# Graph attention with layer norm: the main loop written out, its leaky relu moved onto VectorE alone

## The reference

```
XW = X @ W
s_col = XW @ a[0,:f];  s_row = XW @ a[0,f:]
Z1 = leaky_relu(s_row[:,None] + s_col[None,:], 0.01)
den = exp(Z1)
num = A @ den                                  # 2048 x 2048 x 2048
att = where(num != 0, den / num, 0)            # division by where(num != 0, num, 1)
out = layernorm(x + A @ (att @ XW))
```

## Time and profile before

| | |
|---|---|
| median of 3 runs | 464.31 us (463.53 to 465.45) |
| span of the profiled execution | 463.2 us |
| TensorE busy | 331.5 us (72%) |
| VectorE busy | 317.1 us (68%) |
| ScalarE busy | 198.6 us (43%) |
| GpSimd busy | 188.3 us (41%) |
| chain that ended last | TensorE 50%, VectorE 24%, GpSimd 10% |

### The profile page before, as it was taken

The page is one execution under the profiler, slowest core; times in us unless marked ns, Lnnn a source line. Parts: engine busy times, 40 slices in busy tenths (PEclk is TensorE's granted clock), DMA queues, the critical chain, the costliest instruction groups (busy, mean ns, idle before and its releaser), DMA issues.

```text
span 463.2 us, 7133 instructions
## 1 busy us (share of the span) xinstructions
PE 331.5 (72%) x2214; PEld 166.9 (36%) x2215; DVE 317.1 (68%) x497; ACT 198.6 (43%) x308; POOL 188.3 (41%) x164
## 2 busy tenths in 40 slices
PE   4853718759784333579999999999999840399960
PEld 2553614435561111224343444433444320144420
DVE  0579989998938673869898999975999900201026
ACT  1110022123313474668777777766777840100010
POOL 4000024355555788557454544642556457000000
PEclk9875555697998569689999999999999985599995
DMA  3030043435552325500000000000000041300002
GB/s 111 0 92 2 3 139 95 131 99 178 183 178 74 102 69 150 156 1 0 2 1 0 0 0 0 0 0 0 0 0 0 1 123 52 96 1 0 0 24 68
DMA packets 13877, 24.68 MB, mean 53 GB/s; under 512 B 2080, under 2 KB 8608, under 8 KB 13728
## 3 DMA queue, kind: packets, MB, share of 16 engines
q0 software_dynamic: 5632, 18.88, 13.4%
q1 hardware_dynamic: 8224, 5.51, 4.1%
HBM read 21.23 MB, written 3.15 MB: 53 GB/s over the span
## 4 chain that ended last, share of the span: by engine, by line
PE 50%; DVE 24%; POOL 10%; issue 5%; DMA 5%; ACT 3%; POOLq 0%; SPq 0%; DVEq 0%; ACTq 0%
PE ps L395 17%; PE ps L364 12%; PE ps L424 9%; DVE D L573 5%; DVE D L575 4%; POOL xws L249 3%; POOL d_b L277 3%; PE ps L390 3%; DMA stage<-adjT,perm 3%; PE ps L354 2%; DVE Alo L728 2%; DVE D L579 2%; POOL Alo L233 2%; DVE xws L576 2%; POOL stage L223 2%
## 5 line engine op out<-in xcount | busy, mean ns | idle before, releaser
L267 POOL TENSOR_TENSOR crow<-rrow,cj 128x512 f32<-128x512 f32 x64 | 79.3, 1239 | 79.0 <-DVE crow L751 77.7
L395 PE MATMUL ps<-Ahi,D 128*128 x248 | 87.2, 382 | 2.9 <-issue 1.4
L354 PE MATMUL ps<-Ahi,E 128*96 128x512 f16 x128 | 57.1, 499 | 44.5 <-POOL Alo L233 25.2
L223 POOL DMA_INDIRECT stage<-adjT,perm x32 | 38.9, 1216 | 101.2 <-DVE rs L599 54.6
L754 DVE TENSOR_TENSOR tmp<-crow,tmp 128x512 f32<-128x512 f32 x64 | 65.4, 1022 | 18.3 <-ACT tmp L503 16.5
L364 PE MATMUL ps<-stage,xwp 128*128 128x512 f32 x128 | 71.6, 641 | 2.4 <-DVE stage L741 2.4
L448 ACT CAST Ahi<-stage 128x1024 f16<-128x1024 f32 x32 | 33.2, 1045 | 62.7 <-DMA stage<-adjT,perm 62.2
L424 PE MATMUL ps<-Ahi,D 128*128 128x512 f16 x128 | 40.2, 393 | 24.0 <-DVE D L766 24.0
L501 ACT ACTIVATE tmp<-ps 128x512 f32<-128x512 f32 x64 | 38.1, 595 | 37.7 <-PE ps L397 37.7
L751 DVE SCALAR_TENSOR_TENSOR crow<-crow 128x512 f32<-128x512 f32 x64 | 49.5, 773 | 0.0
L395 PE MATMUL ps<-Alo,D 128*128 x124 | 47.2, 380 | 0.0
(11 more groups left out here) (137 smaller groups left out, 445.5 us busy)
## 6 DMA issues: line engine op xcount, KB each, us to landing
tmp<-xT SPq DMA_DIRECT2D x1, 1024.0 KB, 4.8
d_xw<-stage SPq DMA_DIRECT2D x1, 1024.0 KB, 5.1
xws<-d_b SPq DMA_DIRECT2D x2, 512.0 KB, 4.8
out<-crow SPq DMA_DIRECT2D x4, 256.0 KB, 2.3
stage<-adjT,perm POOLq DMA_INDIRECT x32
xws<-d_xw,perm POOLq DMA_INDIRECT x16
d_b<-crow,ranku POOLq DMA_INDIRECT x16
stage<-wT SPq DMA_DIRECT2D x1, 64.0 KB, 1.9
```

What stands on the lines that cost most here:

```text
L223: nc.gpsimd.indirect_dma_start(out=st[n % NG], out_offset=None, in_=rows, in_offset=bass.IndirectOffsetOnAxis(ap=perm[:, 0, h, b:b + 1], a ...
L267: nc.gpsimd.tensor_tensor(q_t[c % 2], rrow[:, c * W:(c + 1) * W], cj[:, u:u + 1].to_broadcast([P, W]), ALU.add).then_inc(S["q_ready"], 1)
L354: mm = nc.tensor.matmul(ps[0:R, c, :], E[:, e, b, :], a[:, b, c * W:(c + 1) * W], start=(b == 0 and i == 0), stop=(b == NB - 1 and i == 2))
L395: nc.tensor.matmul(num[c], D[:, d, bass.ds(slot, 1), :], a[:, bass.ds(k, 1), c * W:(c + 1) * W], start=False, stop=(i == 2), skip_group_ch ...
```

## The change

TensorE, ScalarE and VectorE get all 16 block columns written out with J as a constant; only the loop over k stays a hardware loop. GpSimd has no part in the main loop any more.

VectorE uses that leaky_relu(r + s) = s + max(r, 0.01 r - 0.99 s). `r01` = 0.01 `rrow` is made once by ScalarE in two halves ahead of the loop, `shift` = -0.99 `cs` once by VectorE. The missing s goes into the bias of the Exp: `ebias` = `cs` + the old bias. One `scalar_tensor_tensor` for a chunk replaces GpSimd's addition and VectorE's old leaky relu. It is placed one chunk ahead: `lz` of chunk t+1, the subtraction of t, `att` of t-1.

The weights matmul is cut into two halves of 256 columns, the first ahead of the k loop, the second behind it in place of the matmul of zeros. `add_bt` reads `xws` itself; the copies into `xwp` go, and the wait for `xws_in` goes from ScalarE to TensorE. The loads of lo and hi stand at the head of every J.

```diff
-                        nc.tensor.matmul(num[c], wgt[0:R, bass.ds(J * P, P)], sums[0:R, c * W:(c + 1) * W],
-                                         start=True, stop=False, skip_group_check=True)
+            for J in range(NB):
+                lo, hi1 = ends_of(J)
+                for c in range(NC):
+                    t = J * NC + c
...
+                    nc.tensor.matmul(num[c][:, 0:HW], wgt[0:R, J * P:(J + 1) * P], sums[0:R, o:o + HW],
+                                     start=True, stop=False, skip_group_check=True)
+                    with pe.Fori(lo, hi1) as k:
...
-                        nc.tensor.matmul(num[c][:, 0:1], z16[:, :], z16[:, 0:1], start=False, stop=True,
-                                         skip_group_check=True).then_inc(S["num_ready"], 1)
+                    nc.tensor.matmul(num[c][:, HW:W], wgt[0:R, J * P:(J + 1) * P], sums[0:R, o + HW:o + W],
+                                     start=False, stop=True, skip_group_check=True).then_inc(S["num_ready"], 1)
+                    if t >= LAG:
+                        add_bt(t - LAG)
```

```diff
 # ScalarE
-            act.wait_ge(S["xws_in"], 16 * NB)
+            wait_lo(act, 2 * NB - 1)
+            act.wait_ge(S["d_z"], NS)
+            for h in range(2):
+                nc.scalar.mul(r01[h], rrow[:, h * H:(h + 1) * H], SLOPE).then_inc(S["r01_sb"], 1)
             act.wait_ge(S["d_lo"], len(BATCH))
+            act.wait_ge(S["shift_sb"], 2)
...
-                            nc.scalar.copy(xwp[:, u, :], xws[:, bass.ds(J * FEAT, FEAT)]).then_inc(S["xwp_ready"], 1)
...
-                nc.scalar.activation(L_t[c], L_t[c], ACT.Exp, bias=sc[:, 4:5]).then_inc(S["exp_done"], 1)
+                nc.scalar.activation(L_t[c], L_t[c], ACT.Exp, bias=ebias[:, J:J + 1]).then_inc(S["exp_done"], 1)
```

```diff
 # VectorE
+            V.tensor_scalar(shift[:, :], cs[:, :], SLOPE - 1.0, None, ALU.mult).then_inc(S["shift_sb"], 1)
+            V.tensor_scalar(ebias[:, :], cs[:, :], sc[:, 4:5], None, ALU.add).then_inc(S["shift_sb"], 1)
...
-                        V.scalar_tensor_tensor(lz_t[c % 2], q_t[c % 2], SLOPE, q_t[c % 2], ALU.mult, ALU.max).then_inc(S["lz_ready"], 1)
+                V.scalar_tensor_tensor(lz_t[t % 2], r01[c // 2][:, c % 2 * W:(c % 2 + 1) * W], shift[:, J:J + 1], rrow[:, c * W:(c + 1) * W],
+                                       ALU.add, ALU.max).then_inc(S["lz_ready"], 1)
```

More of the change, by code:

```diff
@@ L91, in graph_attention_layernorm @@
         a2s = sb("a2s", [P, 2])
-        xwp = sb("xwp", [P, 2, FEAT])
+        shift = sb("shift", [P, NB])
+        ebias = sb("ebias", [P, NB])
         ends = sb("ends", [P, 2, NB])
@@ L121, in graph_attention_layernorm @@
         st = [stage[:, g * H:(g + 1) * H] for g in range(NG)]
-        q_t = [crow[:, 0:W], crow[:, W:2 * W]]
-        lz_t = [crow[:, 2 * W:3 * W], crow[:, 3 * W:4 * W]]
+        lz_t = [crow[:, i * W:(i + 1) * W] for i in range(2)]
+        r01 = [stage[:, 0:H], crow[:, H:N]]
         L_t = [tmp[:, i * W:(i + 1) * W] for i in range(NC)]
@@ L251, in _ @@
                             in_offset=bass.IndirectOffsetOnAxis(ap=perm[:, 1, 2, b:b + 1], axis=0)).then_inc(S["xws_in"], 16)
[L254 to L272, removed]
             for b in range(NB):
@@ L357, in _, with add_bt @@
                     mm.then_inc(S["p_sums"], 1)
-            def add_bt(J, u, c, first, last):
-                t = J * NC + c
+            def add_bt(t):
+                J, c = divmod(t, NC)
                 if c == 0:
-                    pe.wait_ge(S["xwp_ready"], J + 1)
+                    pe.wait_ge(S["xws_in"], 16 * NB)
                 pe.wait_ge(S["att_ready"], t + 1)
-                nc.tensor.matmul(bt[c], xwp[:, u, :], att[c], start=first, stop=last).then_inc(S["bt_added"], 1)
+                nc.tensor.matmul(bt[c], xws[:, J * FEAT:(J + 1) * FEAT], att[c], start=(J == 0), stop=(J == NB - 1)
+                                 ).then_inc(S["bt_added"], 1)
             pe.wait_ge(S["w_lo"], 1)
@@ L368, in _ @@
             LAG = 3
+            HW = W // 2
             def ends_of(J):
[L372 to L379, removed]
-                    else:
[L381 to L389, removed]
-                        nc.tensor.matmul(num[c], wgt[0:R, bass.ds(J * P, P)], sums[0:R, c * W:(c + 1) * W],
-                                         start=True, stop=False, skip_group_check=True)
[L392 to L396, removed]
-                        nc.tensor.matmul(num[c][:, 0:1], z16[:, :], z16[:, 0:1], start=False, stop=True,
-                                         skip_group_check=True).then_inc(S["num_ready"], 1)
-                        if not (first and u == 0 and c < LAG):
-                            pu, pc = divmod(u * NC + c - LAG, NC)
-                            add_bt(J0 + pu, pu % 2, pc, first and pu == 0, last and pu == 1)
@@ L486, in exp_of @@
                 act.wait_ge(S["sub_done"], t + 1)
-                nc.scalar.activation(L_t[c], L_t[c], ACT.Exp, bias=sc[:, 4:5]).then_inc(S["exp_done"], 1)
[L489 to L496, removed]
-                            nc.scalar.copy(xwp[:, u, :], xws[:, bass.ds(J * FEAT, FEAT)]).then_inc(S["xwp_ready"], 1)
[L498 to L510, removed]
+                nc.scalar.activation(L_t[c], L_t[c], ACT.Exp, bias=ebias[:, J:J + 1]).then_inc(S["exp_done"], 1)
+            for t in range(NB * NC):
+                c = t % NC
+                act.wait_ge(S["num_ready"], t + 1)
+                if t >= NC:
+                    act.wait_ge(S["att_ready"], t - NC + 1)
+                nc.scalar.activation(L_t[c], num[c], ACT.Square, scale=1.0 / 256).then_inc(S["sq_done"], 1)
+                act.wait_ge(S["sq_done"], t + 1)
+                nc.scalar.activation(L_t[c], L_t[c], ACT.Ln, bias=epst[:, 1:2]).then_inc(S["ln_done"], 1)
+                if t:
+                    exp_of(t - 1)
@@ L738, in att_of @@
+            def att_of(t):
+                c = t % NC
                 dve.wait_ge(S["exp_done"], t + 1)
-                if not first:
+                if t >= NC:
                     dve.wait_ge(S["bt_added"], t - NC + 1)
                 V.scalar_tensor_tensor(att[c], num[c], 1.0 / 256, L_t[c], ALU.mult, ALU.mult).then_inc(S["att_ready"], 1)
[L743 to L750, removed]
-                        V.scalar_tensor_tensor(lz_t[c % 2], q_t[c % 2], SLOPE, q_t[c % 2], ALU.mult, ALU.max).then_inc(S["lz_ready"], 1)
[L752 to L761, removed]
+            lz_of(0)
+            for t in range(NB * NC):
+                c = t % NC
+                if t + 1 < NB * NC:
+                    lz_of(t + 1)
+                dve.wait_ge(S["lz_ready"], t + 1)
+                dve.wait_ge(S["ln_done"], t + 1)
+                V.tensor_tensor(L_t[c], lz_t[t % 2], L_t[c], ALU.subtract).then_inc(S["sub_done"], 1)
+                if t:
+                    att_of(t - 1)
```

38 lines of the change are left out of this document (25 added, 13 removed).

## The result

The changed kernel takes 451.74 us (median of 4 runs, 450.72 to 452.32) against 464.07 us (463.53 to 465.45). The ratio is 0.9715, 95% interval 0.969 to 0.9741: 12.3 us less. The forecast was 455.4 with a range of 452 to 460. The profiled execution took 450.72 us, the shortest of the four, and its span is 449.0.

The account below looks back on a forecast made before the run. The prediction took TensorE to bound the main loop, VectorE close behind. Its terms -7.0 - 1.1 - 0.9 + 1.6 - 1.5 summed to -8.9 against the 463.2 us span, 454.3; plus 1.1 for the median, 455.4 us, range 452 to 460.

Parts of the forecast that it names:

- late starts and single waits go: TensorE's main loop: twelve late k-loop starts vanish when written out, -7.0 us, and three single waits, -1.1.
- halves for zeros: Weights matmul halves replacing the zeros: -0.015 us a chunk over 60 chunks, -0.9 us, between -1.8 and +3.
- the loop's start: ScalarE's two multiplications ahead of the first Square delay add_bt of chunk 0, +1.1, loads +0.5: +1.6 us (+0.6 to +3.1).
- the loop's end: Block column 15: last Exp at 369.6 instead of 370.99, plus two waits of 0.1: -1.5 us (0 to -2).
- the range's lower end: Whole kernel: 452 us, with stalls gone, the halves at -1.6 and the start at +0.6.
- the 1.1 us of the median: Whole kernel: the median was taken to lie 1.1 us above the profiled span, making 454.3 into 455.4.
- Written out: TensorE's loop with constant J: all twelve late starts in chunks 0 and 3 of even J go, -7.0 us.
- VectorE and GpSimd: Main loop: without GpSimd's 64 additions VectorE needs 2.06 to 2.23 us a chunk, not 2.48; gains slack and 1.1 us of waits.
- rival C: Loop's start: TensorE idles some 2.3 us ahead of add_bt of 0, its clock falls, costing 1.5 us: 456.9; chance 0.17.
- A: Head of each J: loads of lo and hi stay exposed, 7.7 of 8.2 us stay: 463.1; chance 0.09.
- B: Entry of the k loop: TensorE's sequencer becomes the bound, slower; 474 if half of 64 chunks do; chance 0.05.
- D: TensorE's late starts come from the k loop's dynamic start; about half stay, +4 us: 459.4; chance 0.11.

Follow-up runs that it names:

- e2: The changed kernel with one whole weights matmul ahead of the k loop and the one-column matmul of zeros behind it again: 457.16 us, ratio 0.9836.
- e3: The changed kernel with the whole weights matmul back and a matmul of 256 columns of zeros behind the k loop: 458.35 us, ratio 0.9869.
- e1: The kernel before with only the weights matmul in halves, the second replacing the zeros, inside the hardware loop over pairs: 464.67 us, ratio 1.0005.
- e5: The kernel before with only TensorE's loop over pairs written out; zeros, load order and GpSimd's part stay: 455.53 us, ratio 0.9831.
- e6: The changed kernel with TensorE's part, xwp and its copies as before, so the new leaky relu stays and GpSimd is idle: 463.01 us, ratio 0.9996.
- e10: The kernel before with TensorE's loop written out and the weights matmul in halves, old leaky relu with GpSimd's addition kept: 453.45 us, ratio 0.9795.
- e11: The changed kernel unaltered, timed again beside other versions: 451.60 us, ratio 0.9743.
- e4: The changed kernel with ScalarE's two multiplications into r01 moved ahead of its last two copies of sums: 452.61 us, ratio 0.9762.
- e8: The changed kernel with the r01 multiplications ahead of the last two copies of sums, and shift and ebias ahead of the low halves: 451.50 us, ratio 0.9735.

## Why the prediction was right or wrong

| step | forecast | measured | from |
|---|---|---|---|
| late starts and single waits go | -8.1 | -7.2 | 8.2 lost before, 0.95 after, at block columns 10 and 11 |
| halves for zeros | -0.9 | -5.9 in columns 1 to 14 | 0.105 a chunk |
| the loop's start | +1.6 | +1.9 | 1.2 in block column 0, 0.7 in column 1 |
| the loop's end | -1.5 | -1.1 | first scatter |
| sum | -8.9 | -12.3 | |

**The failed step is the term of the halves.** The prediction bounded a chunk's saving by 0.03 us, the distance from the zeros to add_bt, and took 0.015. It measured 0.105. The 0.94 us of add_bt had been read as add_bt's own. 0.084 of it goes when the matmul ahead is long enough, as e2 and e3 show, most likely because the fp32 weight load of add_bt had waited behind a matmul too short to cover it. The trace of the kernel before had the hint, in a view that the prediction doesn't use: two matmuls of one line, one shape and one clock with durations of 592 and 676 ns. The prediction asked what a short first half would do to the weight load behind it, and not what the long second half would do for the weight load behind that. The 0.05 us that it allowed for the first half had no row behind it, and the k loop now starts 0.11 us behind that half, so it costs nothing. The lower bound of -1.8 for this term was therefore no bound. The terms named for the range's lower end (-8.2, -1.6, +0.6, -1.5) give 453.6 with the 1.1 us of the median, not 452, so the range was wider than its own sum and still too short. And the term stood alone in the sum, while the runs show that it is worth nothing inside the hardware loop (e1) and all of its 5.9 us only together with the rest of the change.

By the 262 cycles that the Trainium skill ("TensorE: Matmul & The Clock Gate", Back-to-back issue gap) gives for 256 columns, two halves cost 0.22 us together, an estimate; the trace agrees, 0.11 each. The Trainium skill ("TensorE: Matmul & The Clock Gate", LDWEIGHTS (loading the stationary operand)) gives the columns divided by 1.2 in nanoseconds, from which 128 columns are 0.107 us, an estimate. The exposed 0.084 and the cover of 0.03 add up to about that, and so does the 0.11 between the starts of the two loads; the 0.19 recorded for one load does not.

**Written out.** Right in mechanism and nearly in size. Block column 14's rows were a fair sample of what a constant J does: e5 took away 6.9 us in columns 1 to 14, of which 1.1 are the single waits. What stays in the changed kernel, 0.95, follows the column with three turns of k, where most likely the sequencer has lost its lead by the time it comes to the loads for the next column. The changed kernel's trace there:

```profile
306.95 1.02 PE L342 MATMUL ps<-stage,xws 128*128 128x512 f32 x2
308.02 0.28 PE L364 MATMUL ps<-sums,wgt 96*128 96x256 f16 x1
308.48 0.39 PE L369 MATMUL ps<-Ahi,D 128*128 x1 [0.18 <-issue]
...
309.52 0.39 PE L369 MATMUL ps<-Ahi,D 128*128 x1 [0.22 <-issue]
```

**VectorE and GpSimd.** The subtraction came out as forecast (0.691) and the new leaky relu inside its bounds (0.742, between 0.69 and 0.773), and alone the part gained slack and no time: e6. That the single waits were waits for VectorE, and would go with this part, was wrong; they went with the written-out loop (e5), and two of three stay in e6. In the full change the part may be worth about 2 us (e10 against e11, intervals overlapping), most likely through the sequencer's lead, which the prediction named as cover and didn't price.

**The start.** The sum of +1.6 came near by luck in part. add_bt of 0 begins 6.25 us behind ScalarE's last copy of sums, in both traces of the changed kernel, instead of 5.42: +0.8 and not +1.1. The rest came in another way than it was worked out. In the first trace it was the clock (0.66 over 207 to 212 us, rival C's mechanism), in e11 the missing lead of the sequencer; either made chunk 0 of block column 1 take 3.1 us, and the two don't add to each other. C's price of another 1.5 was too much for the changed kernel, and fits e4 and e8, whose chunk there is 1.4 and 1.2 longer than e11's.

**The end.** -1.1, not -1.5, though the halves took 0.1 us off each chunk here too. Block column 15's chunks on TensorE fell to 1.73 us, and ScalarE, at 1.85 us from one Square to the next, became what sets the pace there, so the last Exp ended 4.05 us behind the start of the last chunk's closing matmul, not 3.1:

```profile
351.76 0.57 ACT L467 ACTIVATE tmp<-ps 128x512 f32<-128x512 f32 x1
...
353.61 0.58 ACT L467 ACTIVATE tmp<-ps 128x512 f32<-128x512 f32 x1
...
356.14 0.72 ACT L460 ACTIVATE tmp<-tmp,ebias 128x512 f32<-128x512 f32 x1 [0.58 <-DVE tmp L726]
```

The rivals A, B and D didn't occur in the change. e1 shows B's ground: with the halves inside the hardware loop late starts take 5.5 of the 5.9 us that the array gains in block columns 1 to 14.

## What to carry to other kernels

Look at what stands ahead of an fp32 weight load: here a matmul too short to cover it made the next one look slow, and two durations in one line at one clock were the sign. Where TensorE's sequencer sets the late places of a loop, first make addresses constants; a faster array pays only after that (e1 gains 0, e5 7.6, both together 10.4, the whole change 12.2 beside the same kernel before). Don't take VectorE for a bound because durations sum to the chunk: see whether it idles (in e10 it did, for 11 us, with 2.44 us of durations in a chunk of 2.38).

## What was not expected of the hardware

255 more columns of zeros were free (0.98 against 0.97 us). In the hardware loop, chunks with loads of two registers ahead of them were late by 0.6 to 1.0 us (chunk 3 of even J); written out, with constant addresses, such chunks weren't late at all but around the column with three turns of k. Useless matmuls in a gap of 2 us cost nothing and the clock didn't fall (one trace).
